# Differential attention: another order of the slot, the output a slot later, weighing on eight tiles, and the gated layer's first steps in its last slots

## What is computed

```python
x = x + _L0_xattn_ref(_layernorm(x), ctx_2048, ...)
x = x + _L0_attn_ref(_layernorm(x), wq, wk, wv, wout, lambda_q1, ..., subln_weight)
x = x + _L0_ffn_ref(_layernorm(x), weight1, weight2, weight3)
x = x + _L1_xattn_ref(...)    # adapter
x = x + _L1_attn_ref(...)
x = x + _L1_ffn_ref(...)

# _L0_attn_ref
q, k = rope(x @ wq.T), rope(x @ wk.T)             # 4 half heads of 64
v = (x @ wv.T).reshape(b, t, 2, 128)
probs = softmax(q @ k.T / SCALING)                # per sequence of 32 rows
diff = probs[:, :, 0] - lam * probs[:, :, 1]
attn = diff @ v
attn = attn * rsqrt(mean(attn * attn) + eps) * subln_weight
return attn @ wout.T

# _L0_ffn_ref, the weights rounded to nf4
h = silu(x @ w1.T) * (x @ w2.T)
return h @ w3.T
```

## Time and profile before

| | |
|---|---|
| median of three runs | 3338.45 us |
| the profiled execution | 3340.0 us |
| its span, first to last instruction | 3338.0 us |
| mean granted TensorE clock | 0.995 of 2.4 GHz |
| busy over the span | PE 99%, PEld 72%, DVE 70%, ACT 60%, POOL 54% |
| first qk matmul of the differential layer | 906.69 us |
| first up matmul of the gated layer | 1099.81 us |

### The profile page before, as it was taken

The page is one execution under the profiler, slowest core; times in us unless marked ns, Lnnn a source line. Parts: engine busy times, 40 slices in busy tenths (PEclk is TensorE's granted clock), DMA queues, the critical chain, the costliest instruction groups (busy, mean ns, idle before and its releaser), DMA issues.

```text
span 3338.0 us, 103494 instructions
## 1 busy us (share of the span) xinstructions
PE 3289.2 (99%) x34656; PEld 2396.0 (72%) x34656; DVE 2338.8 (70%) x7527; ACT 1989.4 (60%) x6064; POOL 1800.7 (54%) x3701
## 2 busy tenths in 40 slices
PE   9999999999899999999999999999999999999999
PEld 7888888888666776777777777777766655555555
DVE  6678887877788667888887888888868844444443
ACT  5777777777556547777777777777765411111111
POOL 5666666666566447777777777777746500000000
PEclk9999999999999999999999999999999999999999
DMA  3111111111211231111111111111136710000000
GB/s 99 54 57 57 55 54 54 56 56 54 72 43 57 88 124 47 46 49 46 47 46 46 46 47 47 47 43 46 49 89 164 199 50 19 19 17 16 17 16 9
DMA packets 280202, 187.70 MB, mean 56 GB/s; under 512 B 117037, under 2 KB 276997, under 8 KB 280085
## 3 DMA queue, kind: packets, MB, share of 16 engines
q1 hardware_dynamic: 275445, 181.55, 19.3%
q10 hardware_dynamic: 4640, 4.59, 0.5%
HBM read 145.61 MB, written 36.21 MB: 54 GB/s over the span
## 4 chain that ended last, share of the span: by engine, by line
PE 59%; DVE 1%; DMA 1%; ACT 0%; issue 0%; POOL 0%; SPq 0%; DVEq 0%; ACTq 0%; POOLq 0%
PE bank_e L2825 13%; PE c_ps_a L1100 7%; PE bank_e L2805 7%; PE b_ps_a L1066 6%; PE s_ps_a L1073 5%; PE out_ps_a L1126 3%; PE a_ps_a L1077 3%; PE c_ps_a L1077 2%; PE b_ps_a L1077 2%; PE out_ps_a L1110 2%; PE c_ps_a L1159 2%; PE m_ps_r L2357 1%; PE c_ps_a L1138 1%; PE out_ps_a L1197 1%; PE c_ps_a L1149 1%; PE m_ps_r L2395 1%
## 5 line engine op out<-in xcount | busy, mean ns | idle before, releaser
L1226 ACT ACTIVATE probs_a<-s_ps_a,neg_max_a 128x257 f32<-128x257 f32 x1024 | 474.4, 476 | 82.2 <-DVE neg_max_a L1346 77.8
L1280 POOL TENSOR_SCALAR probs_a<-probs_a,gated_a 128x256 f32<-128x256 f32 x1024 | 472.3, 482 | 26.3 <-POOL gated_a L1289 26.3
L1346 DVE TENSOR_REDUCE neg_max_a<-s_ps_a 128x1 f32<-128x257 f32 x1024 | 424.0, 414 | 0.0
L2868 ACT ACTIVATE gate_e<-bank_e 128x512 f32<-128x512 f32 x128 | 76.4, 597 | 488.2 <-PE bank_e L2825 461.5
L546 POOL TENSOR_SCALAR probs_i<-probs_i,inv_sum_i 128x256 f32<-128x256 f32 x512 | 244.7, 492 | 132.9 <-DVE inv_sum_i L710 128.5
L2766 POOL TENSOR_TENSOR inv_std_e<-var_eps_e,half_e 128x4 f32<-128x4 f32 x8 | 8.1, 1013 | 563.3 <-DVE var_eps_e L2882 563.3
L2992 DVE TENSOR_TENSOR hidden_e<-gate_e,bank_e 128x512 f32<-128x512 f32 x128 | 87.2, 687 | 282.1 <-PE bank_e L2825 279.4
L1345 DVE TENSOR_TENSOR self_s_a<-s_ps_a,mask_a 128x32 f32<-128x32 f32 x1024 | 185.7, 181 | 134.3 <-PE s_ps_a L1073 134.3
L530 ACT ACTIVATE probs_i<-s_ps_i,neg_max_i 128x257 f32<-128x257 f32 x512 | 236.3, 474 | 59.2 <-DVE neg_max_i L781 57.4
L373 PE MATMUL a_ps_i<-w_k_i,ctx_t_i 128*128 128x256 f32 x1024 | 252.5, 389 | 0.0
L1100 PE MATMUL c_ps_a<-w_v_a,ctx_t_a 128*32 128x256 f32 x4096 | 247.6, 382 | 0.0
(11 more groups left out here) (398 smaller groups left out, 8183.0 us busy)
## 6 DMA issues: line engine op xcount, KB each, us to landing
ctx_t_i<-in_ctx_t SPq DMA_DIRECT2D x128, 256.0 KB, 2.7
ctx_t_a<-in_ctx_t SPq DMA_DIRECT2D x128, 256.0 KB, 2.7
mask_a<-in_L_xattn_mask SPq DMA_DIRECT2D x512, 4.0 KB, 1.5
v_bd_a<-v_self_a SPq DMA_DIRECT2D x512, 8.0 KB, 1.8
x_tok_i<-in_x SPq DMA_DIRECT2D x32, 128.0 KB, 2.0
x_res_i<-in_x SPq DMA_DIRECT2D x32, 128.0 KB, 2.4
x_after<-y_tok_i SPq DMA_DIRECT2D x32, 128.0 KB, 1.8
x_tok_d<-x_after SPq DMA_DIRECT2D x32, 128.0 KB, 2.2
```

Source lines behind the costliest of these rows:

```text
L1226: act.activation(probs[:, t, :], s_ps[:, g, 0:K], ACT.Exp, bias=neg_max[:, t:t + 1], accum_out=row_sum[:, t:t + 1]).then_inc(exp_done, 1)
L1280: pool.tensor_scalar(probs[:, t, 0:2 * P], probs[:, t, 0:2 * P], gated[:, t:t + 1], 1.0, ALU.mult, ALU.mult).then_inc(probs_ready, 1)
L1346: dve.tensor_reduce(neg_max[:, 4 * f + g:4 * f + g + 1], s_ps[:, g, 0:K], AX.X, ALU.max, negate=True).then_inc(max_ready, 1)
```

## The change

It has these parts.

1. TensorE's order within a slot. It was qk, qk_t, v, at, xt, scores, av, y. It is qk, qk_t, xt, v, scores, y, at, av.
2. The output projection and the residual sum of a chunk stand a slot later (n-3 in place of n-2); the layer has one more slot. VectorE's sum waits also for `at_ready`, since y and at now share a bank, as xt and v do.
3. The weighing writes its two heads to different banks (av has two) and the second head to partitions turned by two sequences, so that its eight matmuls use eight different 32x32 tiles. Each of the eight raises `av_full` (four did). ScalarE undoes the turn when it copies `attn_t`, in two instructions in place of one.
4. In the last slots of the layer (31 to 34) TensorE turns the gated layer's weight groups 0 to 5 and its first x, ScalarE copies them, VectorE and GpSimd take the layer norm of a chunk of it in each of the slots 28 to 31. Groups 6 to 8 are turned behind the last slot, and copied by ScalarE between the first steps of turn 0. SyncE's preload stands at slot 26 in place of 30, and the loads of the second turn's x and of the residual at slot 34.

The diff, cut:

```diff
-    qk_ps, v_ps, tx_ps, av_ps = (pb(f"{n}_ps") for n in ("qk", "v", "tx", "av"))
-    s_ps = pb("s_ps", (P, 2, 512))
-    qk_t_ps, y_ps = (pb(f"{n}_ps") for n in ("qk_t", "y"))
+    qk_ps, qk_t_ps, vx_ps, ya_ps = (pb(f"{n}_ps") for n in ("qk", "qk_t", "vx", "ya"))
+    av_ps, s_ps = (pb(n, (P, 2, 512)) for n in ("av_ps", "s_ps"))
...
-    SLOTS = range(-3, CHUNKS + 3)
+    SLOTS = range(-3, CHUNKS + 4)
...
     def sync(sp, ahead):
         for n in SLOTS:
-            if n == CHUNKS - 2:
+            if n == CHUNKS - 6:
...
+            if n == CHUNKS + 2:
+                ahead.second(sp)
+            if live(n - 3):
...
     def tensor(pe, before, ahead):
+        def weigh(n):
+            if live(n - 1):
+                pe.wait_ge(diff_ready, n)
+                pe.wait_ge(v_ready, n)
+                ge(pe, attn_ready, n - 1)
+                for s in range(4):
+                    own = slice(L * s, L * s + L)
+                    for c in range(2):
+                        across = (s + 2 * c) % 4
+                        last = pe.matmul(av_ps[L * across:L * across + L, c, 0:P], diff_t[(n - 1) % 2][own, c * L:c * L + L], v[(n - 1) % 3][own, c * P:c * P + P], start=True, stop=True)
+                        last.then_inc(av_full, 1)
...
         for n in SLOTS:
+            if n == CHUNKS - 1:
+                pe.wait_ge(qk_read, CHUNKS)
+                ahead.weights[0](pe, 0)
+                pe.wait_ge(v_ready, CHUNKS)
+                ahead.weights[0](pe, 1)
+            if n == CHUNKS:
+                ahead.weights[0](pe, 2)
+                ahead.weights[0](pe, 3)
...
+            if live(n + 2):
+                pe.wait_ge(xn_ready, n + 3)
+                ge(pe, xn_t_ready, n + 2)
+                ge(pe, v_ready, n + 1)
+                for c in range(2):
+                    last = pe.transpose(xt_ps[:, c * P:c * P + P], xn[:, c * P:c * P + P], ident[:, :])
+                last.then_inc(x_full, 1)
             if live(n + 1):
                 ge(pe, v_ready, n + 1)
+                ge(pe, xn_t_ready, n + 2)
...
+            if n < CHUNKS - 1:
+                scores(n)
+                output(n)
+            else:
+                output(n)
+                scores(n)
+            if n == CHUNKS:
+                weigh(n)
+                pe.wait_ge(qk_t_ready, CHUNKS)
+                ahead.weights[0](pe, 4)
...
+            if n == CHUNKS:
+                ahead.weights[0](pe, 5)
+                pe.wait_ge(centred_ready, CHUNKS)
+                ahead.rows[0](pe, 0)
+            elif n == CHUNKS + 1:
+                ahead.rows[0](pe, 1)
+            else:
+                weigh(n)
...
+                act.activation(attn_t_of[:, 0::3, :], at_of[:, 0::2, :], ACT.Copy)
+                act.activation(attn_t_of[:, 1:3, :], at_of[:, 1::2, :], ACT.Copy).then_inc(at_ready, 1)
...
+            if n + 4 - CHUNKS in range(LANES):
+                ahead.lanes[0](dve, n + 4 - CHUNKS)
+            if n == CHUNKS + 2:
+                ahead.rows[2](dve)
+            if live(n - 3):
+                if live(n - 2):
+                    dve.wait_ge(at_ready, n - 1)
+                dve.wait_ge(y_full, n - 2)
...
-    W_TURNS = 3 * (PARTS + 1)
+    W_BANKS = [bank[0], bank[2], bank[0], bank[2], bank[1], bank[0], down_ps[0], down_ps[0], down_ps[1]]
+    W_BEFORE = [None, None, 0, 1, None, 2, None, None, None]
...
+    def tensor(pe, before, ahead):
+        for group in range(6, 9):
+            turn_weights(pe, group)
...
             for n in range(PARTS + 1):
                 silu(i, n)
+                if i == 0 and n < 3:
+                    copy_weights(act, 6 + n)
```

More of the change, by code:

```diff
@@ L180 @@
     pool: Callable = None
+    weights: tuple = ()
+    rows: tuple = ()
+    lanes: tuple = ()
 def image_attention(nc, io, stack):
@@ L1635, in tensor, with scalar, normalized @@
                 last.then_inc(at_full, 1)
[L1636 to L1659, removed]
-                        last = pe.matmul(av_ps[own, c * P:c * P + P], diff_t[(n - 1) % 2][own, c * L:c * L + L], v[(n - 1) % 3][own, c * P:c * P + P], start=True, stop=True)
-                        if c == 1:
-                            last.then_inc(av_full, 1)
-            if live(n - 2):
-                if n - 2 == 0:
-                    pe.wait_ge(w_o_ready, 1)
-                pe.wait_ge(at_ready, n - 1)
-                ge(pe, y_ready, n - 2)
-                for c in range(2):
-                    last = pe.matmul(y_ps[:, 0:D], attn_t[:, c, :], w_o[:, c, :], start=c == 0, stop=c == 1)
-                last.then_inc(y_full, 1)
-    def scalar(act):
-        for n in SLOTS:
+            if n == CHUNKS:
[6 more added lines that the diff above has]
+                weigh(n)
+    def scalar(act, ahead):
+        def normalized(n):
             if live(n - 2):
@@ L1676, in scalar, with squared @@
                 for h in range(2):
-                    last = act.activation(attn[:, h, :], av_ps[:, h * P:h * P + P], ACT.Copy, scale=inv_rms[:, h:h + 1])
+                    last = act.activation(attn[:, h, :], av_ps[:, h, 0:P], ACT.Copy, scale=inv_rms[:, h:h + 1])
                 last.then_inc(attn_ready, 1)
+        def squared(n):
+            if live(n - 1):
+                act.wait_ge(av_full, 8 * n)
+                for h in range(2):
+                    last = act.activation(squares[:, h, :], av_ps[:, h, 0:P], ACT.Square, accum_out=ss[:, h:h + 1])
+                last.then_inc(ss_ready, 1)
+        for n in SLOTS:
+            if n == CHUNKS - 1:
+                ahead.weights[1](act, 0)
+            if n == CHUNKS:
+                ahead.weights[1](act, 2)
+                ahead.weights[1](act, 3)
             if live(n + 1):
@@ L1926, in turn_x @@
[L1926 to L1929 removed]
+                turn_half_x(pe, c, i)
         def wait_bank(i, tile):
@@ L1959, in tensor @@
                 wait_bank(i, tile)
+                if i == 0 and tile == 3:
+                    pe.wait_ge(*before.high)
                 for c in range(2):
@@ L2139, in vector @@
             if ahead:
-                low_of_x(i + 1)
+                low_of_x(dve, i + 1)
         adapter_statistics(1)
```

251 lines of the change are left out of this document (154 added, 97 removed).

## The result

The changed kernel takes 3368.19 us (median of 4 runs, 3362.95 to 3369.29) against 3338.77 us before: ratio 1.0087, 95% interval 1.0076 to 1.0099. It is slower by 29.4 us; the forecast was 15.6. The direction and the ring were right, the forecast size was about half of the measured one.

A forecast was written before the change was run, and what follows sets the result against it. TensorE was taken as the bound at 5.38 us a slot; a new ring of waits makes it 5.93. 14.9 (27 slots) + 0.4 (filling) + 0.1 (end) = +15.4, giving 3354 us; own range 3350 to 3361, 8 in 10 3342 to 3361.

The forecast's parts named there:

- TensorE gains nothing alone: Steady slot: 0.19 us saved in the weighing is spent on one more tile-shape change, so TensorE's sum stays 5.38 us.
- the longer one: Ring from weighing through squares, `ms`, `xn`, xt, v, scores, y, at: 5.93 us a slot (5.88 to 6.07), +14.9 us.
- the shorter: Ring from scores through row maxima, `xn`, xt and v back to the scores: 5.52 us a slot.
- rival (a): Weighing: eight tiles take turns in pairs, weighing stays 0.57, ring 6.07, +19.1 us, 3357.5 us; chance 0.08.
- (b): Steady slot: squares don't hold `ms`, only the 5.52 us ring stands, +4.3 us in all, 3343 us; chance 0.07.
- (c): Steady slot: `xn` is in time, no ring binds, slot 5.19 us, 3328 us; chance 0.08.
- (d): Steady slot: `xn` is in time but the slot stays 5.38 us, -5.3 us, 3333 us; chance 0.04.
- weighing to squares at 0.65: First link of the longer ring: 0.79 us before, 0.60 with the 0.19 less, taken as 0.65.
- the end of the layer at +0.1: Last qk to first up matmul: 24.0 us becomes 24.1, the 6.6 us saved given back by the longer drain.
- the clock at 0: End of the layer and gated turn 0: half-clock stretches might cost up to +3.5 us, but were counted as 0.
- later layers at 0: Layers behind the differential one: no term for them in the sum, forecast difference 0.
- filling: First four steps of the layer: v of chunk 1 must wait for `xn` of chunk 2, +0.4 us.

The follow-up runs named there:

- e5: The change with TensorE's xt put behind the scores instead of ahead of v: 3357.42 us, ratio 1.0055.
- e1: The change with VectorE's mean square `ms` moved behind `xn`: 3349.02 us, ratio 1.0028.
- e2: The change with one increment of `av_full` for the eight weighing matmuls in place of eight: 3360.65 us, ratio 1.0064.
- e6: The change with five needless fp32 matmuls in TensorE's longest waits of slots 30 to 32: 3362.70 us, ratio 1.0076.
- e8: The kernel before with 11 needless fp32 matmuls behind the last y of the differential layer: 3354.55 us.
- e9: The kernel before with 26 needless fp32 matmuls behind the last y of the differential layer: 3366.65 us.
- g1: The change reordered: TensorE qk, v, qk_t, y, xt, scores, av, at; VectorE's residual sum before row maxima, ScalarE's squares before exponentials: 3346.36 us, ratio 1.0024.
- g2: g1 with GpSimd's sine part waiting for VectorE's `xn`, and the last slots written out with no copies before the attention's normalization: 3330.05 us, ratio 0.9976.

## Why the prediction was right, and where not

**Right.** TensorE gains nothing alone: e5 less its one wait is 5.37, forecast 5.38. Two rings, the longer one through the weighing, the squares, `ms` and `xn`: it measures 6.04, inside its range of 5.88 to 6.07, and cutting it at `ms` (e1) leaves the shorter, 5.48 for a forecast of 5.52. The eight tiles work at the same time (av to qk 0.38), so rival (a) is out; the Trainium skill's sentence that weight loads overlap only in another row group (TensorE: Matmul & The Clock Gate, The mechanism) does not bring about that wait here. Rivals (b), (c) and (d) would have needed slots of 5.52, 5.19 and 5.38 and none came; the first of them is what e1 had to build.

**The first step that failed: weighing to squares at 0.65.** It is 0.74. I took the row with the passes taken off and counted the increments as a small rest, though the Trainium skill's price, which I quoted, gave 0.72. e2 shows that price. The ring is then 6.04 and not 5.93, in 27 slots +3.0; another 0.9 is the single slot of 6.91.

**The second: the end of the layer at +0.1, with the clock at 0.** The drain was added up at the full-clock durations, and the half clock given an end of +3.5 that I did not put into the sum. Measured +4.0; e6 puts 2.8 on the clock. The waits that I had listed myself before each y (1.38 and 2.65 us in the first two rows of the last stretch) are what TensorE did before the clock fell.

**The third, and the largest: later layers at 0.** They cost 5.0 in the profiled execution (6.4 in the reshaped attention, less 1.4 on the way there). Nothing in the sum allowed for it, nor in the range, and no reason was given for the 0. e8 shows that a delay alone can cost this much; whether the change's 5.0 come from its delay stays open, since e9 reached the layer 1.2 us sooner and its trace shows 163.9. What the change's trace has in place of the 0 is 4.9 us more of ScalarE's waits for `k_rows` (17.8 for 12.9) and 6.8 us at half clock. These 5.0 are the greater part of why the range, up to 3361, did not hold 3368: of the 7 us above it they are 5.0 and the start 1.5, while the slots (+18.8 for an end of +18.6) and the last stretch (+4.0, its clock priced up to +3.5) nearly kept to their own ends. The 1.5 us of start lie before the layer; first qk lies between 905.2 and 908.2 in these traces, so they are scatter.

Sum of what was missed: 3.9 + 3.9 + 5.0 + 1.5 + 0.3 (filling), less 0.55 (turn 0), is 14.0; span 29.5 less 15.4 forecast is 14.1.

## What to carry to other kernels

When an operation moves to another place of a software-pipelined slot, add up every ring of waits that closes through it, with the strict queues of the other engines as links, before counting what the moved engine saves; and look for the one order in which no ring is above the busy engine's own sum. A small instruction in the middle of a busy queue (here `ms`) ties two chains together. Work handed to idle time must not stand ahead of the last item's own path, and a delay need not be neutral for what follows: the kernel before, held back by 9.3 us, became 15.9 us longer. An untouched layer is no constant in the sum: look at its scatter over several runs before giving it a 0.

## What the runs showed of the hardware

- An increment on a matmul tile costs 27 ns on the way to the waiting engine (e2: seven fewer, 0.19 us), although the weighing's records stay 0.45.
- VectorE and GpSimd block each other by who begins first: a 128x512 product of two SBUF operands takes 0.69 us on VectorE when it begins first and 1.33 when a sine part is already running (g1); GpSimd's sine half takes 0.84 alone and 1.17 to 1.36 behind the cosine part (g2, before). The Trainium skill (SBUF — State Buffer, Who interferes with whom) states that a VectorE instruction with two SBUF inputs contends with a GpSimd instruction that reads SBUF, and that the ports which they share are an exclusive lock. The trace agrees: in g1 the cosine part, begun 0.11 after the second sine half, ends at 1010.02, 0.55 after that half's end at 1009.47.
- Filling TensorE's waits with needless matmuls shortened a stretch from 28.0 to 25.25 us, since the granted clock stayed at its full level (1.00 in place of 0.76 over it).
- The same code of a layer took 162.6 to 172.9 us in thirteen traces. The longer ones have longer waits of ScalarE for the DMAs of `k_rows` (14.6 to 17.8 us in all, against 12.7 to 13.2). In the two longest, of different programs that reach it 0.3 us apart, a stretch at half clock lies at the same place (from 2518.8).
